# Summing attention weights over keys: four half-width products with ones per group, against one vector addition and one full-width product

## The reference

```python
h = _layernorm(x)
mod = jax.nn.silu(time) @ mod_w + mod_b          # time: (16, 1, 512)
shift, scale, gate = jnp.split(mod, 3, axis=-1)
h = h * (scale + 1.0) + shift
qkv = (h @ w_qkv).reshape(B, T, 3, H, e).transpose(2, 0, 3, 1, 4)
q, k, v = (qkv[0], qkv[1], qkv[2])
q = _apply_rope(_layernorm(q, q_norm_w), position)
k = _apply_rope(_layernorm(k, k_norm_w), position)
scores = jnp.einsum('bhqe,bhke->bhqk', q, k) / jnp.sqrt(jnp.asarray(e, q.dtype))
attn = jax.nn.softmax(scores, axis=-1)
o = jnp.einsum('bhqk,bhke->bhqe', attn, v)
x = x + o @ w_out * gate
```

## Time and profile before

| | |
|---|---|
| median of three runs | 1744.09 us |
| profiled execution | 1738.36 us |
| span of its instructions | 1736.6 us |
| PE busy | 1669.5 us, 96% of the span |
| DVE busy | 1247.1 us, 72% |
| ACT busy | 1034.1 us, 60% |
| POOL busy | 680.7 us, 39% |
| products with ones, L475 | 2016 records, 161.9 us busy |
| POOL's accumulating DMAs, L1315 | 126, 1 MB each, 7.7 us median to landing |

### The profile page before, as it was taken

The page is one execution under the profiler, slowest core; times in us unless marked ns, Lnnn a source line. Parts: engine busy times, 40 slices in busy tenths (PEclk is TensorE's granted clock), DMA queues, the critical chain, the costliest instruction groups (busy, mean ns, idle before and its releaser), DMA issues.

```text
span 1736.6 us, 34608 instructions
## 1 busy us (share of the span) xinstructions
PE 1669.5 (96%) x13350; PEld 1007.4 (58%) x13350; DVE 1247.1 (72%) x1667; ACT 1034.1 (60%) x1610; POOL 680.7 (39%) x707
## 2 busy tenths in 40 slices
PE   5978899999999999999999999999999999999887
PEld 3734556665666666666566666666656666665444
DVE  8767677777777777777777777777777777776553
ACT  3445666666666666566666666666666666665552
POOL 0523243344344344334434434433443443443322
PEclk9979999999999999999999999999999999999999
DMA  6034355554645555555555555555555546454553
GB/s 214 25 68 85 82 129 113 134 116 110 137 113 125 125 122 119 119 127 117 122 125 126 112 130 117 119 131 116 122 116 126 131 107 143 104 113 107 128 122 110
DMA packets 55432, 204.48 MB, mean 118 GB/s; under 512 B 6872, under 2 KB 6872, under 8 KB 39144
## 3 DMA queue, kind: packets, MB, share of 16 engines
q0 software_dynamic: 18144, 132.13, 39.1%
q1 hardware_dynamic: 37128, 70.14, 12.0%
HBM read 53.25 MB, written 16.88 MB: 40 GB/s over the span
## 4 chain that ended last, share of the span: by engine, by line
PE 92%; DVE 5%; issue 1%; DMA 1%; POOL 1%; ACT 0%; SPq 0%; ACTq 0%; DVEq 0%; POOLq 0%
PE O L459 13%; PE SA L440 13%; PE Y L345 12%; PE Y L358 10%; PE Y L348 9%; PE Y L352 9%; PE Y L475 8%; PE SM L397 6%; PE MB L380 3%; PE SA L444 3%; PE SA L335 1%; PE SA L418 1%; DVE cst L1074 1%; DVE cst L1066 1%; PE MB L408 1%
## 5 line engine op out<-in xcount | busy, mean ns | idle before, releaser
L819 ACT ACTIVATE probs<-SM 128x1024 f32<-128x1024 f32 x256 | 262.3, 1025 | 235.1 <-PE SM L444 226.3
L1066 DVE TENSOR_REDUCE cst<-SM 128x2 fp32r<-128x1024 f32 x236 | 289.1, 1225 | 153.4 <-PE MB L397 153.4
L1315 POOL DMA_DIRECT2D probs<-probs x126 | 109.8, 871 | 594.0 <-ACT probs L821 541.1
L1066 DVE TENSOR_REDUCE cst<-MB 128x2 fp32r<-128x1024 f32 x236 | 287.0, 1216 | 0.0
L459 PE MATMUL O<-probs,vals 128*32 128x512 f32 x2048 | 270.9, 601 | 0.0
L1296 POOL TENSOR_TENSOR pair_part<-rows,rope_pair 128x256 f32<-128x256 f32 x128 | 119.6, 935 | 382.8 <-DVE rows L1043 381.9
L821 ACT ACTIVATE probs<-SA 128x1024 f32<-128x1024 f32 x256 | 262.4, 1025 | 0.0
L345 PE MATMUL Y<-wqkv_hi,hT_hi 128*128 128x512 f32 x716 | 215.4, 423 | 0.0
L715 ACT ACTIVATE rows<-Y 128x512 f32<-128x512 f32 x121 | 72.4, 599 | 205.0 <-PE Y L352 205.0
L348 PE MATMUL Y<-wqkv_hi,hT_lo 128*128 128x512 f32 x716 | 193.9, 392 | 0.5 <-DVE hT_lo L1049 0.5
L1055 DVE SCALAR_TENSOR_TENSOR qk_lo<-MB,pass_w,qk_hi 128x512 fp32r<-128x512 f32 x128 | 90.3, 746 | 144.8 <-ACT qk_hi L751 144.7
(11 more groups left out here) (221 smaller groups left out, 3557.0 us busy)
## 6 DMA issues: line engine op xcount, KB each, us to landing
probs<-probs POOLq DMA_DIRECT2D x126, 1024.0 KB, 7.7
xin<-in_x_dram SPq DMA_DIRECT2D x62, 256.0 KB, 7.4
xres<-in_x_dram SPq DMA_DIRECT2D x60, 256.0 KB, 2.6
out_dram<-xres SPq DMA_DIRECT2D x60, 256.0 KB, 5.7
shift_scale<-mod_rows SPq DMA_DIRECT2D x15, 512.0 KB, 3.7
gate<-mod_rows SPq DMA_DIRECT2D x16, 256.0 KB, 5.4
rows<-in_L_cond_mod_w_dram SPq DMA_DIRECT2D x2, 1024.0 KB, 9.0
probs<-in_L_cond_w_qkv_dram SPq DMA_DIRECT2D x2, 1024.0 KB, 13.3
```

What stands on the lines that cost most here:

```text
L819: act.activation(probs[:, a, 2:4, :], SM[:], ACT.Exp).then_inc(s_exp, 1)
L1066: dve.tensor_reduce(heads[:, 2 * half:2 * half + 2, 0], bank[:], AX.X, ALU.max, negate=True).then_inc(max_out, 1)
```

## The change

The two DMAs stay. DVE then adds the buffer that holds tiles 0 and 1 to the one that holds tiles 2 and 3 (`sum_keys`, one instruction over 2048 elements per partition, in place), and PE makes one product with ones over all 512 queries per group (`add_over_keys(g)`), behind `scores_by_key(s, 2)` of the next step. ACT's two copies and DVE's two half additions go, the logarithm reads the bank Y directly and moves between the two exponentials of key tile 2. The buffers rotate by one place in the ring (0, 1, 3, 2) from group to group, and ACT's waits before the exponentials change with that.

```diff
+    PROBS_RING = (0, 1, 3, 2)
+
     def probs_buffer(g, t):
-        return t ^ (g % 2)
+        return PROBS_RING[(PROBS_RING.index(t) + g) % TT]
...
-            def add_over_keys(g, t, h):
-
-                pe.wait_ge(first_added if t == 0 else second_added, 16 * (g + 1))
-                if h == 1 or t == 2:
-                    pe.wait_ge(first_summed, 2 * g + (1 if t == 0 else 2))
-                if h == 1 and t == 2:
-                    pe.wait_ge(sum_added, 2 * g + 1)
-                if t == 0 and h == 0 and g > 0:
-                    pe.wait_ge(sum_added, 2 * g)
-                cols = half_cols(h)
+            def add_over_keys(g):
+
+                pe.wait_ge(keys_summed, g + 1)
                 for i in range(HG):
-                    mm = pe.matmul(Y[head_rows(i), cols], ones_r[:, 0:E].bitcast(F32),
-                                   probs[:, probs_buffer(g, t), i, cols],
+                    mm = pe.matmul(Y[head_rows(i), :], ones_r[:, 0:E].bitcast(F32),
+                                   probs[:, probs_buffer(g, 2), i, :],
                                    start=True, stop=True, skip_group_check=True)
                 mm.then_inc(ones_done, 1)
...
                 scores_by_key(s, 0)
                 if s > 0:
-                    if tile(s + 5):
-                        pe.wait_ge(raw_out, raw_count(s + 5, 1))
-                    if s == LAST:
-                        pe.wait_ge(y_gated, NT - TT - 1)
-                    add_over_keys(s - 1, 0, 1)
                     weigh_values(s - 1, 3)
...
-                if s > 0:
-                    if tile(s + 4):
-                        pe.wait_ge(v_out, s + 5)
-                    add_over_keys(s - 1, 2, 0)
                 weigh_values(s, 0)
...
                     if n >= 0:
                         pe.wait_ge(y_gated, n + 1)
-                    add_over_keys(s - 1, 2, 1)
+                    else:
+                        pe.wait_ge(v_out, s + 5)
+                    add_over_keys(s - 1)
                 weigh_values(s, 1)
...
                     if s > 0:
-                        pe.wait_ge(sum_added, 2 * s)
+                        pe.wait_ge(sum_ln, s)
                     else:
                         pe.wait_ge(v_out, s + 5)
                     project(s + 6, 0, Y[:])
...
-                if group(s + 1):
-                    if tile(s + 6):
-                        pe.wait_ge(raw_out, raw_count(s + 6, 0))
-                    add_over_keys(s, 0, 0)
                 weigh_values(s, 2)
...
-                    if g > 0:
-                        act.wait_ge(pv_step, TT * (g - 1) + (t ^ 1) + 1)
...
+                    if g > 0 and t == 0:
+                        act.wait_ge(pv_step, TT * (g - 1) + 2)
+                        act.wait_ge(first_added, 16 * g)
+                    elif g > 0 and t == 1:
+                        act.wait_ge(pv_step, TT * g)
+                        act.wait_ge(second_added, 16 * g)
+                    elif g > 0 and t == 2:
+                        act.wait_ge(keys_summed, g)
+                    elif g > 0:
+                        act.wait_ge(ones_done, g)
...
                 key_exponentials(s, 0, 0)
-                if s > 0:
-                    move_first_sum(s - 1, 1)
                 key_exponentials(s, 0, 1)
...
                 key_exponentials(s, 2, 0)
+                if s > 0:
+                    log_sums(s - 1, Y[:])
                 key_exponentials(s, 2, 1)
                 if s > 0:
-                    log_sums(s - 1, sum_inv[:])
                     inverse_sums(s - 1)
...
                 key_exponentials(s, 3, 0)
-                if s < LAST:
-                    move_first_sum(s, 0)
                 key_exponentials(s, 3, 1)
...
-            def add_sums(g, h):
-                dve.wait_ge(ones_done, 4 * g + 3 + h)
-                dve.wait_ge(first_summed, 2 * g + 1 + h)
-                cols = half_cols(h)
-                dve.tensor_tensor(sum_inv[:, cols], sum_inv[:, cols], Y[:, cols], ALU.add).then_inc(sum_added, 1)
+            def sum_keys(g):
+                dve.wait_ge(first_added, 16 * (g + 1))
+                dve.wait_ge(second_added, 16 * (g + 1))
+                total, part = (probs[:, probs_buffer(g, t)].rearrange("p h n -> p (h n)") for t in (2, 0))
+                dve.tensor_tensor(total, total, part, ALU.add).then_inc(keys_summed, 1)
...
                 if tile(s + 5):
                     square_sums(s + 5, 1)
+                if s > 0:
+                    sum_keys(s - 1)
                 if late(s + 1):
                     late_maxima(s + 1, 1, 0)
-                if s > 0:
-                    add_sums(s - 1, 0)
-                if late(s + 1):
                     late_maxima(s + 1, 1, 1)
...
-                if s > 0:
-                    add_sums(s - 1, 1)
```

More of the change, by code:

```diff
@@ L151, in cond_attention_kernel @@
             sem("x_scaled"), sem("h_lo"), sem("qk_low"), sem("max_out"), sem("o_scaled"), sem("y_gated"))
-        sum_added, pass_set = sem("sum_added"), sem("pass_set")
+        keys_summed, pass_set = sem("keys_summed"), sem("pass_set")
         o_high, o_low, last_high, last_low, wout_low = (
@@ L577, in _ @@
                 if s > 0 and tile(s + 4):
-                    pe.wait_ge(first_summed, 2 * s)
+                    if s > 1:
+                        pe.wait_ge(sum_ln, s - 1)
+                    if tile(s + 5):
+                        pe.wait_ge(raw_out, raw_count(s + 5, 1))
                     project(s + 4, 2, Y[:])
@@ L601, in _ @@
                     pe.wait_ge(o_low, n + 1)
-                    pe.wait_ge(sum_added, 2 * s - 1)
+                    pe.wait_ge(sum_ln, s - 1)
+                    if tile(s + 4):
+                        pe.wait_ge(v_out, s + 5)
+                    if s == LAST:
+                        pe.wait_ge(y_gated, NT - TT - 1)
                     project_out(n, Y[:], 0, 4)
@@ L641, in _ @@
                     add_last_sums(2)
-                    pe.wait_ge(sum_added, 2 * LAST)
+                    pe.wait_ge(sum_ln, LAST)
                     project_last(1, 0, 2)
@@ L650, in _ @@
                     pe.wait_ge(o_low, NT - TT - 1)
-                    pe.wait_ge(first_summed, 2 * s + 1)
+                    pe.wait_ge(sum_ln, s)
                     project_out(NT - TT - 2, Y[:], 0, 12)
                 if tile(s + 6):
-                    pe.wait_ge(first_summed, 2 * s + 1)
+                    pe.wait_ge(raw_out, raw_count(s + 6, 0))
                     project(s + 6, 1, Y[:])
@@ L767, in output_high, with log_sums @@
                 act.activation(o_hi[:], tile_out(n), ACT.Copy).then_inc(o_high, 1)
-            def move_first_sum(g, h):
-                act.wait_ge(ones_done, 4 * g + h + 1)
+            def log_sums(g, sums):
+                act.wait_ge(ones_done, g + 1)
                 if g > 0:
@@ L774, in move_first_sum @@
                     act.wait_ge(parts_out, 3)
-                cols = half_cols(h)
-                act.activation(sum_inv[:, cols], Y[:, cols], ACT.Copy).then_inc(first_summed, 1)
-            def log_sums(g, sums):
-                if g < LAST:
-                    act.wait_ge(sum_added, 2 * g + 2)
-                else:
-                    act.wait_ge(ones_done, 4 * g + 1)
-                    act.wait_ge(o_scaled, g)
                 act.activation(sum_inv[:], sums, ACT.Ln).then_inc(sum_ln, 1)
@@ L793, in key_exponentials @@
                     act.wait_ge(s_done, n + 1)
-                    if g > 0:
-                        act.wait_ge(pv_step, TT * (g - 1) + (t ^ 1) + 1)
-                    if t == 0:
-                        if g > 0:
-                            act.wait_ge(first_added, 16 * g)
-                        else:
-                            act.wait_ge(w_low[0], 1)
+                    if g > 0 and t == 0:
[8 more added lines that the diff above has]
+                        act.wait_ge(ones_done, g)
+                    elif t == 0:
+                        act.wait_ge(w_low[0], 1)
                     elif t == 1:
-                        if g > 0:
-                            act.wait_ge(ones_done, 4 * g - 2)
-                        else:
-                            act.wait_ge(w_low[1], 1)
+                        act.wait_ge(w_low[1], 1)
                     elif t == 2:
-                        if g > 0:
-                            act.wait_ge(second_added, 16 * g)
-                        else:
-                            act.wait_ge(mod_partial, 3)
-                    elif t == 3:
-                        if g > 0:
-                            act.wait_ge(ones_done, 4 * g)
-                        else:
-                            act.wait_ge(wout_low, 1)
+                        act.wait_ge(mod_partial, 3)
+                    else:
+                        act.wait_ge(wout_low, 1)
                 a = probs_buffer(g, t)
```

4 lines of the change are left out of this document (removed).

## The result

The change makes the kernel slower. Four runs gave 1757.07 us in the median (1754.19 to 1761.31), against 1744.16 (1743.22 to 1744.54) of the kernel before: a ratio of 1.0077, with a 95% interval of 1.0053 to 1.0101. The prediction, 1707 us, has the wrong sign. The profiled execution has a span of 1752.4 us (1736.6 before).

The account below looks back on a forecast made before the run. PE was taken to bound the kernel; -0.5 (step 0), -2.4 (steps 1 to 4), -41.9 (middle) and +7.8 (late) sum to -37.0 us, from 1744.1 to 1707 us, range 1690 to 1722.

Parts of the forecast that it names:

- What hides the rest of a middle step: Middle steps: ACT's logarithm has cover of 0.5 us, the DMA costs nothing, removed ACT copies beside PE give nothing.
- what is taken off PE is time gained: Steps 5 to 57: work removed from PE shortens the step, as far as the other engines keep up.
- What goes from PE: Each step: four half-width calls of 0.46 us become one of 0.88, 0.96 us less.
- The term -41.9: Steps 5 to 57: 53 steps, each 0.79 us shorter, -41.9 us in all.
- What comes to DVE: The new addition over 2048 elements on DVE takes 2.3 us, between 2.13 and 5.1.
- (c): Addition slowed by POOL to 5.1 us in each of 62 steps: 1881 us, slower than before; chance 0.05.
- (d): Addition takes 2.5 to 2.6 us for an unseen reason, such as DMA traffic: +14, 1721 us; chance 0.10.
- The race to `scores_by_key(s, 2)`: Middle steps: PE comes 0.92 us earlier and is held 0.17 us for `x_low`, so the step gains 0.79.
- rival (a): Middle steps: PE is not held for `x_low` at all, 9 us more gained, 1698 us; chance 0.18.
- Steps 1 to 4: Early steps, bound by DVE's chain at `x_low`: -0.60 us each, -2.4 in all.
- The late steps: Steps 58 to 62: addition ahead of tile 1's maxima; +1.0 for step 58, +1.7 each for 59 to 62, +7.8 us.
- rival (b): Late steps: the clock falls after PE's idle time, 1.7 us per fall, five times: 1715 us; chance 0.14.

Follow-up runs that it names:

- e8: Changed kernel with a half-width product with ones put back ahead of three value products in steps 2 to 57: 1783.31 us.
- e4: Kernel before the change with its four products with ones cut from 256 to 32 columns each: 1707.47 us.
- e3: Changed kernel with ACT's first exponential of each key tile halved, so bank SM is free sooner (wrong data): 1727.59 us.
- e1: Changed kernel with DVE's addition moved behind the maxima of tile 1 in late steps: 1743.02 us, 1.0011 of before.
- e2: Changed kernel with DVE's addition over 256 of 2048 elements, sums incomplete: 1739.98 us.
- e7: e1 with one projection matmul ahead of scores by query of tiles 0, 1, 3, and x's statistics and transposes earlier: 1730.41 us, 0.9923 of before.
- e9: e7 with half-width products with ones ahead of three value products in steps 58 to 62 only: 1731.56 us, 0.9928 of before.
- e5: Changed kernel with the buffers of the kernel before in place of the four-way rotation: 1930.42 us.

## Why the prediction was wrong

**The step that failed** is "What hides the rest of a middle step". It takes up ACT's logarithm and its wait for the second DMA, and then says that ACT's removed copies lie beside PE. It does not ask what PE's calls wait for once they come earlier. `scores_by_query` has a wait of its own, for `s_exp`, ACT's first exponential of the tile in hand: PE writes the bank SM that ACT reads. In step 28 of before that wait showed no idle time, because the product with ones stood between. From rows that were on record it could have been read how close it was. For key tile 1 ACT's exponential ended at 826.83 + 1.02 = 827.85, PE can start 0.15 behind such an end (the prediction's own figure, from the earlier trace rows), at 828.00, and it started at

```profile
828.13 0.50 PE L397 MATMUL SM<-qk_hi 32*128 32x512 f32 x2
```

That is a margin of 0.13 us for a product of 0.46. The margin cannot be won back by coming earlier, since ACT's exponential follows the key scores, which stand ahead of the removed product (it starts as far behind the start of the key scores' last rows in both kernels: 826.83 behind 826.38 before, 825.70 behind 825.26 after). That is also why "what is taken off PE is time gained", the first paragraph's premise, did not hold: its condition, "as far as the other engines keep up", was looked up for `x_low` and not for this wait. PE without idle time shows that nothing waits now, and no more.

**What goes from PE**, 0.96 us a step by the sum: right in size, wrong in effect. Three of the four calls gave 0.46 - 0.32 = 0.14 each, 0.42 in all, and the wider product at the fourth place took that back: in step 28 it took 0.89 us from start to start instead of 0.46, so 0.43. The step stayed where it was. The term -41.9 was -0.2 (the start of step 58 less that of step 5: 1353.27 after, 1353.44 before). e8, e4 and e3 show this from three sides: the products put back, the products thinned in the kernel before, and ACT's hold on SM shortened.

**What comes to DVE**, 2.3 us: measured 2282 ns, against 2.28 worked out. Rivals (c) and (d) fell with it. What (c) feared did not come near it: none of the 63 additions had a computation of POOL beside it, and what one would do to it no run here shows. Nor had it POOL's DMA beside it in step 28, where the next was issued only at 827.94, behind the addition's end at 827.60. In the late steps of e1 such a DMA did stand beside it, and there it took 2.28 us all the same. It waited for a DMA for 1.6 us in the whole run. That the addition costs the middle nothing is shown by e2.

**The race to `scores_by_key(s, 2)`**: not reached in the changed kernel, since PE never came that early. Where it is reached, in e3, PE is held for 0.18 us against 0.17 predicted, the step is 24.78 against 24.75, and rival (a), 24.58, is out.

**Steps 1 to 4** took 106.5 us together instead of 106.2, +0.3 where -2.4 was forecast. It is the same failed step. In step 2, which starts at 151.66 before and at 150.34 after, the two pairs of maxima start at

```profile
156.11 1.23 DVE L1066 TENSOR_REDUCE cst<-SM 128x2 fp32r<-128x1024 f32 x1 [0.55 <-PE MB L397]
162.07 1.23 DVE L1066 TENSOR_REDUCE cst<-SM 128x2 fp32r<-128x1024 f32 x1 [0.86 <-PE MB L397]
```

```profile
154.67 1.23 DVE L1037 TENSOR_REDUCE cst<-SM 128x2 fp32r<-128x1024 f32 x1 [0.43 <-PE MB L395]
160.56 1.22 DVE L1037 TENSOR_REDUCE cst<-SM 128x2 fp32r<-128x1024 f32 x1
```

Within the step the first came 0.12 us earlier (4.33 instead of 4.45), not 0.46, because PE's scores had waited for ACT, and so the second came 0.19 earlier instead of 0.56; behind them the wider product cost its 0.43 and the call taken away near the step's end gave 0.14. In sum that is +0.1 a step. Step 0 took 27.56 us instead of 28.61, but 28.67 in e1, which has the same program there, so the -0.46 of that step lies within what one execution differs from another.

**The late steps**, +7.8 us: measured +17.4. The place and the kind were right, and so, but for the clock, was about the size. "PE's next half starts at 1641.85 instead of 1640.80" puts it 10.47 us behind the start of step 60 (1631.38) instead of 9.42. In step 61 of the changed kernel it starts 12.00 us behind (1674.79 behind 1662.79), which is 10.5 once the 1.5 of the slower clock are taken off; in the same way the whole step is 1.5 us longer than before, against +1.7. What came on top is rival (b)'s fall of the clock, in every late step. As an estimate: step 61 lost 1.5 us at a mean granted clock of 0.93; the five steps have 0.88, 0.88, 0.93, 0.93 and 0.93, and in proportion to what is missing to 1.00, times the step's length, they lost about 10.5 us together. That leaves +6.9 for all else. The rival's price of 1.7 us per fall was near. I gave it a chance of 0.14 as a case beside the forecast, where it was part of every late step, and I let step 3, which had once kept 1.00 after such an idle time, speak against it.

**The chances.** 0.06 for slower was too little for another reason too: each rival had the gain of the middle steps in it, so all of them rested on the premise that failed. A rival that takes the gain itself away was missing.

**What stays open**: why the clock falls in the late steps of e1, e7 and e9 and not in those of the kernel before, with idle times of like length. It may be that it falls there too in other executions: the one that was profiled took 1738.36 us, the others between 1738.00 and 1750.04 at mean granted clocks of 0.983 to 0.990, and where in them the clock fell isn't on record.

## What to carry to other kernels

Before counting work taken off the busiest engine as time, list for each call behind it every wait that it has, and from the trace when each of them was met; the smallest of those margins is the most that the call can gain, however much work is removed. An instruction that ends no wait may still be the cover of one, and a cover is worth as much as the wait that it hides. Where two engines alternate on one buffer, even a short instruction belongs behind the exchange, and what is ahead of it costs its time and, in the late steps here, as much again by the slower clock.

## What the runs showed of the hardware

- One 128x512 matmul between products that use 32 rows or columns took 0.43 us from start to start, in a row of its kind 0.26 to 0.27 (1.02 / 4, 0.81 / 3): one such matmul set apart from its row cost PE 0.22 us more.
- VectorE's addition of 2048 float32 elements per partition took 2282 ns on average. In a middle step no accumulating DMA is under way beside it (step 28: the next is issued at 827.94, the addition ends at 827.60). In the five late steps of e1 one is, from before the addition's start until behind its end, and it took 2281 to 2283 ns there. One of the five, with POOL's issue beside it too:

```profile
1667.47 2.28 DVE L1052 TENSOR_TENSOR probs<-probs 128x2048 f32<-128x2048 f32 x1
```

```profile
1667.27 0.87 POOL L1284 DMA_DIRECT2D probs<-probs  x1 [8.14 <-ACT probs L795]
```

- The granted clock fell below 1 in most, but not all, of the steps with an idle time of 1.8 to 2.2 us on PE: in e5, 16 of the middle steps with the same wait of 2.2 us kept 1.00 (27.5 us), nearly all the others had 0.94 (29.0 us). It also fell in late steps of e1, e7 and e9, where no idle time was longer than 1.33 us.
